# Cross-attention with layer norm: K and V two batches ahead, Q in four groups, the first shift in halves, maxima split behind their transpose

## The chip, the cores and the metric

One core of one Trainium2 chip runs the whole kernel. The metric is the device time in microseconds (us) of one execution. Names: PE is TensorE, DVE is VectorE, ACT is ScalarE, POOL is GpSimd, SP is SyncE, which here only issues transfers.

## The reference

Eight batches, 112 queries, 375 keys, model width 256, 16 heads of 16:

```python
def _attention(query, key_value, W_qkv, b_qkv, W_o, b_o, ln_gamma, ln_beta):
    ...
    Q = (query @ Wq.T + bq).reshape(B, Sq, N_HEADS, D_K).transpose(0, 2, 1, 3)
    K = (key_value @ Wk.T + bk).reshape(B, Skv, N_HEADS, D_K).transpose(0, 2, 1, 3)
    V = (key_value @ Wv.T + bv).reshape(B, Skv, N_HEADS, D_K).transpose(0, 2, 1, 3)
    scores = jnp.einsum('bhqd,bhkd->bhqk', Q.astype(jnp.float32), K.astype(jnp.float32))
    scores = scores / np.sqrt(D_K)
    attn = jax.nn.softmax(scores, axis=-1)
    context = jnp.einsum('bhqk,bhkd->bhqd', attn, V.astype(jnp.float32)).astype(query.dtype)
    context = context.transpose(0, 2, 1, 3).reshape(B, Sq, D_MODEL)
    output = context @ W_o.T + b_o
    x = output + query
    mu = jnp.mean(x, axis=-1, keepdims=True)
    var = jnp.mean(jnp.square(x - mu), axis=-1, keepdims=True)
    return (x - mu) / jnp.sqrt(var + LN_EPS) * ln_gamma + ln_beta
```

## The kernel before, in words

Every engine's program is one list of instructions, written out by the Python code and taken in order; semaphores join the lists. There is no planner: constants say in which unit of a batch a piece of work stands.

**Precision.** Matmul operands for scores and projections are pairs of a rounded high part and a low part (value minus high part), and a product is three matmuls: high by high, high by low, low by high. For the scores the three sit in one contraction: `k_stack` (three buffers, batch b in b % 3) holds high, low, high in every fourth partition, `q_stack` high, high, low. The fourth lane of `k_stack` is filled with ones, and the lanes facing it in `q_stack` take the negated maximum of each query row, the **shift** (its high and its low part). So the softmax's subtraction happens in the matmul.

**Two passes over the scores.** `scores_for_max(n)` (L834; n = 16 b + h is a *head*) computes one head of queries by keys into one of three PSUM banks, and DVE's `head_max(n)` (L656) reduces it to the negated maximum. `negate` (L663, L665) splits the maxima of a batch in high and low part, PE transposes them (`transpose_max`, L841), DVE copies them out of PSUM (`take_shift`, L672) and a transfer issued by ACT puts them in `q_stack` (L520). Then `shifted_scores(i, u)` (L857) computes keys by queries for four heads and a third of the keys: a **unit**, 12 in a batch. ACT takes the exp (L561), and `values` (L873) multiplies with V, which has a column of ones for the denominator; two groups of four heads at a time, in units 1 and 7. The result is copied (`take_o`, L535), transposed (`transpose_o`, job OT, L884), normalised on DVE, transposed back (ONT, L893), copied by ACT (L552), projected (`out_project`, L901) and normalised by row: statistics and rescaling on DVE, the power, gamma and beta on POOL.

**Projections.** `k_project` (two halves of 8 heads a batch), `v_project` (three key chunks) and `q_project` all record line L793. K's half goes through ACT (high part with the bias, L474), DVE (low part, L627) and three transfers of SP into `k_stack` (`stack_k`, L302). Q comes in three groups: batch 0, batches 1 to 4, 5 to 7. The context is split by a cast (L457 on ACT, later L612 on DVE) and a subtraction (L606 on DVE, L359 on POOL).

**Order.** Before batch 0 PE works through 20 heads with Q group 1, V of batch 1, K and V of batch 2 between them (`EARLY_HEADS`, `EARLY_JOBS`). Then `MAX_HEADS` adds 21 heads to the units of batch 0 and 16 to each later batch, and batch i projects K and V of batch i + 3 (`AHEAD`), K in units 0 and 2, V in 3, 5 and 8. Maxima of batch i + 1 are complete by unit 4 or 5 of batch i; the transpose is in unit 7, the shift's transfer behind the exp of unit 9. In batch i stand also OT of batch i - 1 (unit 5), ONT (9) and the output projection (11).

**Banks.** Small results share PSUM banks; `JOBS` lists the order of the jobs of each bank, and `claim` waits until the job before in the same bank has been read (`last_read`).

Of the kernel before, what the change touches and what calls it, by code (L numbers as in the profile page):

```python
# [22 lines left out]
F32 = mybir.dt.float32  # L23
# [9 lines left out]
NC = 3  # L33
# [5 lines left out]
GB = 4  # L39
# [3 lines left out]
Q_STACKS = ((0, 1), (1, 1 + GB), (1 + GB, B))  # L43
# [5 lines left out]
AHEAD = 3  # L49
# [3 lines left out]
Q1_SPLIT = 5  # L53
# [13 lines left out]
EARLY_HEADS = H + 4  # L67
EARLY_JOBS = {1: ("Q", 1, 0), 3: ("Q", 1, 1), 5: ("V", 1, 0), 7: ("V", 1, 1), 9: ("V", 1, 2), 11: ("K", 2, 0),
              13: ("K", 2, 1), 14: ("V", 2, 0), 15: ("V", 2, 1)}


M0_JOBS = [("K", 0, 0), ("V", 0, 0), ("Q", 1, 0), ("K", 2, 0)]
M1_JOBS = [("K", 0, 1), ("V", 0, 1), ("Q", 1, 1), ("K", 2, 1)]
S0_JOBS = [("Q", 0, 0), ("K", 1, 0), ("V", 1, 0), ("MT", 0), ("V", 2, 1)]
S1_JOBS = [("Q", 0, 1), ("K", 1, 1), ("V", 1, 1), ("V", 2, 0)]
for _i in range(B):
    if _i + AHEAD < B:
        M0_JOBS += [("K", _i + AHEAD, 0), ("V", _i + AHEAD, 0), ("V", _i + AHEAD, 1)]
        M1_JOBS.append(("K", _i + AHEAD, 1))
    if _i == 0:  # L80
        M1_JOBS += [("BIAS",), ("Q", 2, 0)]
    if _i >= 1:
        M1_JOBS.append(("OT", _i - 1))
    if _i + 1 < B:
        M1_JOBS.append(("MT", _i + 1))
    if _i == 0:
        M1_JOBS.append(("Q", 2, 1))
    if _i >= 1:
        M1_JOBS += [("ONT", _i - 1), ("OUT", _i - 1)]
M0_JOBS += [("OT_HALF", 0), ("ONT_HALF", 0)]  # L90
M1_JOBS += [("OT_HALF", 1), ("ONT_HALF", 1)]
# [13 lines left out]
def build(nc, x_nat, xT, ctxT, wT, woT, b_cols, bv_cols, b_o, gamma, beta, out):  # L105
    ctx = ExitStack()
    with ctx:
# [63 lines left out]
        shift_in = [sem(f"shift_in{i}") for i in range(2)]  # L171
        stored = [sem(f"stored{i}") for i in range(2)]
# [23 lines left out]
        WIDE = UNITS * (B - 2) + UNITS // 2  # L196
# [15 lines left out]
        def m_job(*job):  # L212
# [35 lines left out]
        def stack_q(queue, k, side):  # L248
# [4 lines left out]
            queue.wait_ge(q_clear[k], 2 if k == 1 else 1)  # L253
# [12 lines left out]
        def _(sp):  # L266
# [76 lines left out]
        def _(pool):  # L343
# [702 lines left out]
```

## Time and profile before

| what | value |
|---|---|
| median of 3 runs | 156.24 us (154.76 to 158.16) |
| profiled execution, time | 157.02 us |
| its span | 155.2 us, granted clock 0.982 on average |
| PE busy | 134.0 us (86%), 1466 matmuls |
| DVE busy | 105.6 us (68%) |
| ACT busy | 80.4 us (52%) |
| POOL busy | 60.7 us (39%) |
| first maximum on DVE starts | 17.1 us |

The span goes from the first to the last instruction; the profiled execution's time is 1.8 us more. Times in rows are us from the span's start. A matmul's busy time overlaps the next one's, so the distance of two starts is the better price. The granted clock is TensorE's, as a share of 2.4 GHz. Batch 3 begins at 82.7 us, batch 5 at 112.6, batch 6 at 123.85 and batch 7 at 135.8.

### The profile page before, as it was taken

Reading aid. Unit: us, or ns where it says so; the run is one execution under the profiler, and the core shown is the slowest. Engines: PE = TensorE matmul, PEld = TensorE weight load, DVE = VectorE, ACT = ScalarE, POOL = GpSimd, SP = SyncE. Lnnn points to the kernel's source line nnn. Section 1 sums busy time; section 2 is a strip of 40 time slices with the busy share of each in tenths; the row PEclk is TensorE's granted clock in tenths of the full one; section 3 lists DMA queues with packets and bytes.
Section 4 is the critical chain, followed back from the end, with each engine's and each line's share of the span. In section 5 each row is a group of like instructions: output and inputs, shape, how many; then the busy total and the mean of one; then the engine's idle time right before and its main releaser. Section 6 shows DMA issues by size and latency. Waiting matters only on the chain.

```text
span 155.2 us, 3853 instructions
## 1 busy us (share of the span) xinstructions
PE 134.0 (86%) x1466; PEld 116.7 (75%) x1466; DVE 105.6 (68%) x247; ACT 80.4 (52%) x163; POOL 60.7 (39%) x83
## 2 busy tenths in 40 slices
PE   5799989679979999889998998999899996779850
PEld 4599779468768899769988987899787875667620
DVE  6745997757937769947896699578779887031252
ACT  3648437214426666526655666465656565566410
POOL 8946997920003998404140504130023023041051
PEclk9999999987999999999999999999999999999997
DMA  4976989698950250697414050405031001001002
GB/s 128 358 259 216 269 296 227 159 270 239 301 204 2 102 156 0 169 267 235 135 52 151 4 178 4 155 2 183 24 128 34 4 4 30 4 4 30 4 0 59
DMA packets 14354, 19.58 MB, mean 126 GB/s; under 512 B 2192, under 2 KB 13520, under 8 KB 14336
## 3 DMA queue, kind: packets, MB, share of 16 engines
q1 hardware_dynamic: 13056, 17.26, 35.6%
q0 software_dynamic: 592, 1.70, 4.5%
q10 hardware_dynamic: 688, 0.38, 0.8%
q8 instruction: 12, 0.20, 0.5%
q14 instruction: 6, 0.05, 0.1%
HBM read 6.30 MB, written 0.92 MB: 47 GB/s over the span
## 4 chain that ended last, share of the span: by engine, by line
PE 65%; DVE 11%; DMA 10%; ACT 6%; issue 5%; SPq 1%; POOLq 0%; ACTq 0%; DVEq 0%
PE m_bank L793 19%; PE pv_bank L873 12%; PE st_bank L857 11%; PE mx_bank L834 10%; DMA q_stack<-shift 6%; DVE mx L656 6%; PE m_bank L901 4%; DMA c_raw<-ctxT 3%; PE m_bank L884 2%; ACT pw L561 2%; PE st_bank L793 2%; DMA q_stack<-q_first 1%; DVE q_hl L618 1%; PE m_bank L841 1%; ACT o_normT L552 1%
## 5 line engine op out<-in xcount | busy, mean ns | idle before, releaser
L656 DVE TENSOR_REDUCE mx<-mx_bank 112x1 f32<-112x375 f32 x128 | 64.6, 541 | 20.4 <-PE mx_bank L834 19.8
L561 ACT ACTIVATE pw<-st_bank 125x448 f32<-125x448 f32 x90 | 48.5, 548 | 48.5 <-PE st_bank L857 47.7
L834 PE MATMUL mx_bank<-k_stack,q_stack 128*112 128x376 f32 x128 | 41.3, 351 | 2.2 <-DVE mx L656 1.2
L857 PE MATMUL st_bank<-q_stack,k_stack 128*125 128x224 f32 x180 | 37.7, 294 | 1.7 <-DMA q_stack<-shift 1.7
L857 PEld LDWEIGHTS st_bank<-q_stack,k_stack 128*125 128x125 f32 x180 | 30.0, 190 | 5.5 <-issue 3.0
L834 PEld LDWEIGHTS mx_bank<-k_stack,q_stack 128*112 128x112 f32 x128 | 22.0, 181 | 4.5 <-DVE mx L656 2.4
L359 POOL TENSOR_TENSOR c_hl<-c_raw,c_hl 128x752 fp32r<-128x752 f32 x6 | 10.9, 1814 | 27.5 <-DVE c_hl L612 27.5
L873 PE MATMUL pv_bank<-pw,v_sb 125*17 125x112 f32 x720 | 20.4, 260 | 1.1 <-ACT o_raw L535 1.1
L405 POOL TENSOR_SCALAR var_eps<-mv 112x1 f32<-112x1 f32 x7 | 1.6, 223 | 49.2 <-DVE mv L692 49.2
L793 PE MATMUL m_bank<-c_hl,w_hl 128*128 128x376 f32 x84 | 18.7, 365 | 0.9 <-ACT w_hl L449 0.9
L873 PEld LDWEIGHTS pv_bank<-pw,v_sb 125*17 125x17 f32 x720 | 16.3, 97 | 3.9 <-issue 2.2
L793 PEld LDWEIGHTS m_bank<-c_hl,w_hl 128*128 128x128 f32 x84 | 16.5, 212 | 1.6 <-ACT c_hl L457 1.6
L793 PE MATMUL m_bank<-w_hl,c_hl 128*125 128x256 f32 x108 | 15.8, 285 | 0.0
L793 PEld LDWEIGHTS m_bank<-w_hl,c_hl 128*125 128x125 f32 x108 | 14.4, 186 | 0.0
L627 DVE SCALAR_TENSOR_TENSOR k_hl<-m_bank,bqk,k_hl 128x376 fp32r<-128x376 f32 x14 | 8.4, 606 | 4.4 <-ACT k_hl L474 4.4
L901 PE MATMUL m_bank<-wo,o_normT 128*112 128x256 f32 x28 | 7.6, 396 | 3.5 <-ACT o_normT L552 3.5
L474 ACT ACTIVATE k_hl<-m_bank,bqk 128x376 fp32r<-128x376 f32 x14 | 8.0, 570 | 2.5 <-PE m_bank L793 2.5
L901 PEld LDWEIGHTS m_bank<-wo,o_normT 128*112 128x112 f32 x28 | 4.4, 176 | 5.5 <-ACT o_normT L552 4.8
L416 POOL TENSOR_TENSOR yo<-z,g_rows 112x256 f32<-112x256 f32 x7 | 5.1, 734 | 7.5 <-DVE z L696 7.5
L688 DVE TENSOR_TENSOR z<-m_bank,x_space 112x256 f32<-112x256 f32 x7 | 2.9, 417 | 6.3 <-PE m_bank L901 6.3
L485 ACT COPY v_sb<-m_bank 125x512 f32<-125x512 f32 (+1 forms) x12 | 5.7, 478 | 1.5 <-issue 1.0
L793 PE MATMUL m_bank<-q_stack,w_hl 128*128 128x448 f32 (+1 forms) x24 | 5.0, 344 | 1.3 <-DVE bo_rows L635 1.3
(102 smaller groups left out, 160.6 us busy)
## 6 DMA issues: line engine op xcount, KB each, us to landing
k_stack<-k_hl SPq DMA_DIRECT2D x48, 188.0 KB, 2.5
c_raw<-ctxT SPq DMA_DIRECT2D x8, 375.0 KB, 4.3
q_stack<-q_hl SPq DMA_DIRECT2D x6, 224.0 KB, 4.5
q_stack<-q_hl SPq DMA_DIRECT2D x6, 168.0 KB, 3.4
x_space<-x_nat POOLq DMA_DIRECT2D x1, 896.0 KB, 10.3
out<-yo SPq DMA_DIRECT2D x8, 112.0 KB, 1.9
pw<-wT SPq DMA_DIRECT2D x2, 256.0 KB, 4.8
x_space<-xT SPq DMA_DIRECT2D x1, 448.0 KB, 6.1
```

What stands on the lines that cost most here:

```text
L359: nc.gpsimd.tensor_tensor(c_hl[b % 2][:, 1, :, :], c_raw[b % 2][:, :, :], c_hl[b % 2][:, 0, :, :].bitcast(F32), op=ALU.subtract).then_inc( ...
L416: nc.gpsimd.tensor_tensor(yo[b % 2][:, :], z[b % 2][:, :], g_rows[:, :], op=ALU.mult).then_inc(y_scaled, 1)
L474: nc.scalar.activation(k_hl[b % 2][:, 0, t, :], src[:, 0:KVP], ACT.Identity, bias=bqk[:, 2 + t:3 + t]).then_inc(k_hi, 1)
L485: nc.scalar.copy(v_sb[b % VR][0:KC, c0:c0 + chunks, :, 0:DK], src[0:KC, 0:chunks * D].rearrange("p (c h d) -> p c h d", c=chunks, h=H)).th ...
L561: nc.scalar.activation(p_tile[0:KC, n % PR, :, :], st_of(n)[0:KC, 0:4 * Q].rearrange("p (j q) -> p j q", j=4), ACT.Exp, scale=float(DK) ** ...
L627: nc.vector.scalar_tensor_tensor(out=k_hl[b % 2][:, 1, t, :], in0=m_bank[m][:, 0:KVP], scalar=bqk[:, 2 + t:3 + t], in1=k_hl[b % 2][:, 0, t ...
L656: nc.vector.tensor_reduce(mx[b % 2][:, h % 2, q_pair(h // 2):q_pair(h // 2) + 1], mx_bank[n % MR][0:Q, 0:KV], axis=AX_X, op=ALU.max, negat ...
L793: last = nc.tensor.matmul(dst, lhs(a, e), rhs(c, e), start=(k + e == 0), stop=(k == len(PRODUCTS) - 1 and e == EC - 1))
L834: nc.tensor.matmul(mx_bank[n % MR][0:Q, 0:KVP], q_stack[k][:, side, q_pair(h // 2), b - Q_STACKS[k][0], :], k_stack[b % 3][:, h // 2, :], ...
L857: last = nc.tensor.matmul(st_of(n)[0:KC, k * 2 * Q:(k + 1) * 2 * Q], k_stack[i % 3][:, 2 * g + k, c * KC:(c + 1) * KC], q_stack[qk][:, :, ...
L873: last = nc.tensor.matmul(pv_of(b, g)[32 * j:32 * j + VW, g * Q:(g + 1) * Q], v_sb[b % VR][0:KC, c, 4 * g + j, :], p_tile[0:KC, (UNITS * b ...
L901: last = nc.tensor.matmul(dst[0:Q, D:2 * D], o_normT[b % 2][:, k, :], wo[:, k, :], start=(k == 0), stop=(k == EC - 1))
```

## The change

- `AHEAD` is 2: batch i projects K and V of batch i + 2, K in units 3 and 5 (4 and 6 in batch 0), V in units 9, 10 and 11. Early heads are 14; K and V of batch 2 are projected in batch 0.
- K's half is read from PSUM once by ACT into `k_full`; ACT copies the high part from there and POOL subtracts the low part. (For the first two batches it is as before.) `stack_k` of a batch waits for all scores of the batch whose buffer it takes.
- The context's high part moves from DVE (unit 7) to ACT (unit 2), and stays one batch ahead of its projection.
- Q has four groups: batch 0, 1 to 2, 3 to 5, 6 to 7.
- Maxima are transposed as they are, and DVE splits them out of PSUM. In later batches their transpose is one job with ONT of batch i - 2. The shift is two transfers issued by SP, one for each part. Batch 0's shift is taken in two halves of 8 heads, the first behind head 9, the second in unit 1 (transfers issued by ACT).
- Output projections and layer norms stand about a batch later: unit 2 of batch i for batch i - 3. The rescaling moves to POOL, the value bias to batch 1.

```diff
-Q_STACKS = ((0, 1), (1, 1 + GB), (1 + GB, B))
+Q_STACKS = ((0, 1), (1, 3), (3, 6), (6, B))
-AHEAD = 3
+AHEAD = 2
-U_K = (0, 2)
-U_V = (3, 5, 8)
-U_OT, U_ONT, U_OUT = 5, 9, 11
-U_BIAS = 4
-U_Q = (5, 10)
-U_NEGATE, U_MT, U_SHIFT = 5, 7, 9
-U_CONTEXT = 7
-HEADS = (1, 1, 2, 1, 2, 1, 1, 1, 2, 1, 2, 1)
+U_OUT, U_OT, U_BIAS, U_Q = 2, 6, 1, 1
+U_K = ((4, 6), (3, 5))
+U_V = ((9, 10, 11), (10, 11, 9))
+NORM_WITH = {3: 0, 4: 1, 5: 2, 6: 3, 7: 5}
+U_MT = (10, 8, 8, 8, 8, 8, 8)
+EARLY_HEADS = 14
+EARLY_JOBS = {1: ("Q", 1, 0), 3: ("Q", 1, 1), 5: ("V", 1, 0), 7: ("V", 1, 1), 9: ("MT", 0, 0), 10: ("V", 1, 2)}
+FIRST_JOBS = {1: (("MT", 0, 1),), 7: (("Q", 2, 0),), 8: (("Q", 2, 1),)}
+HEADS = (2, 2, 2, 1, 2, 1, 2, 1, 1, 1, 1, 0)
+FIRST_HEADS = ((2, 1, 2, 2, 2, 2, 2, 2, 2, 2, 2, 1),)
...
-                    sp.wait_ge(st_full, UNITS * (b - 3) + UNITS // 2 * (t + 1))
+                    sp.wait_ge(st_full, UNITS * (b - 2))
...
+            def stack_shift(b):
+                k = q_stack_of(b)
+                to = q_stack[k][:, :, :, b - Q_STACKS[k][0], :].rearrange("p s a q -> p (s a) q")
+                sp.wait_ge(shift_ready, b + 2)
+                for part in range(2):
+                    row = SPREAD * (part + 1) - 1
+                    sp.dma_start(to[row:row + 1, :, :].bitcast(F32),
+                                 shift[b % 2][:, part, :].bitcast(F32)).then_inc(shift_in[b % 2], 16)
             for i in range(B):
                 if i + AHEAD + 2 < B:
                     load_context(i + AHEAD + 2)
+                if i == 4:
+                    for side in range(2):
+                        stack_q(sp, 3, side)
+                if i + AHEAD < B:
+                    for t in range(2):
+                        stack_k(i + AHEAD, t)
+                if i + 1 < B:
+                    stack_shift(i + 1)
+                if i == 0:
+                    for side in range(2):
+                        stack_q(sp, 2, side)
+                if i >= 3:
+                    store(i - 3)
... (POOL, in its loop)
+            for i in range(B - AHEAD):
+                if i >= 1 and i + AHEAD + 1 < B:
+                    context_lo(i + AHEAD + 1)
+                for t in range(2):
+                    subtract_k(i + AHEAD, t)
+                if i == 0:
+                    context_lo(AHEAD + 1)
... (ACT)
+            def take_k(b, t):
+                src = wait_full(act, "K", b, t)
+                if b > AHEAD:
+                    act.wait_ge(k_lo, 2 * (b - 1) + t + 1)
+                nc.scalar.activation(k_full[:, t, :], src[:, 0:KVP], ACT.Identity,
+                                     bias=bqk[:, 2 + t:3 + t]).then_inc(k_taken, 1)
+                act.wait_ge(k_taken, 2 * (b - AHEAD) + t + 1)
+                act.wait_ge(k_in[(b - 2) % 3][t], 48 * ((b - 2) // 3 + 1))
+                nc.scalar.copy(k_hl[b % 2][:, 0, t, :], k_full[:, t, :]).then_inc(k_hi, 1)
... (DVE)
+            def split_shift(src, to, n):
+                nc.vector.tensor_copy(to[:, 0, :], src).then_inc(shift_hi, 1)
+                dve.wait_ge(shift_hi, n)
+                nc.vector.tensor_tensor(to[:, 1, :], src, to[:, 0, :].bitcast(F32), op=ALU.subtract).then_inc(shift_ready, 1)
... (PE, in shifted_scores)
-                if u == 0:
-                    pe.wait_ge(shift_in[i % 2], 16 * (i // 2 + 1))
+                if i == 0 and u % HALF == 0:
+                    pe.wait_ge(half_in[u // HALF], 32)
+                if i >= 1 and u == 0:
+                    pe.wait_ge(shift_in[i % 2], 32 * ((i + 1) // 2))
```

## Rows read from the trace of the kernel before

**Rows 1.** From the page: the chain that ended last, shares by engine.

```profile
PE 65%; DVE 11%; DMA 10%; ACT 6%; issue 5%; SPq 1%; POOLq 0%; ACTq 0%; DVEq 0%
```

**Rows 2.** Stretches: busy PE, PEld, DVE, ACT, POOL; PEclk, DMA share, GB/s.

```profile
82.70:97.66 14.96, 14.37 (x180) 13.05 (x178) 11.83 (x28) 8.68 (x18) 4.10 (x5) 1.00 0.25 87
112.60:123.85 11.25, 10.90 (x150) 9.01 (x148) 9.90 (x25) 6.67 (x14) 2.24 (x4) 1.00 0.16 55
123.85:135.80 11.95, 9.40 (x141) 7.66 (x139) 6.24 (x18) 6.69 (x14) 2.25 (x4) 1.00 0.04 12
135.80:155.20 19.40, 12.16 (x192) 8.98 (x190) 6.14 (x19) 7.65 (x18) 5.02 (x9) 0.95 0.07 19
28.00:33.00 5.00, 2.39 (x14) 1.53 (x13) 3.66 (x9) 0.96 (x2) 4.00 (x7) 1.00 0.75 193
33.67:37.08 3.41, 3.41 (x15) 3.20 (x14) 1.67 (x4) 1.37 (x3) 0.00 (x0) 0.51 0.92 229
```

**Rows 3.** Timeline of PE in batch 3: start, length, line, idle before it.

```profile
84.74 1.34 PE L873 MATMUL pv_bank<-pw,v_sb 125*17 125x112 f32 x48
86.02 0.48 PE L857 MATMUL st_bank<-q_stack,k_stack 128*125 128x224 f32 x2
...
86.50 1.18 PE L793 MATMUL m_bank<-c_hl,w_hl 128*128 128x376 f32 x6
87.53 0.33 PE L834 MATMUL mx_bank<-k_stack,q_stack 128*112 128x376 f32 x1
87.70 0.37 PE L857 MATMUL st_bank<-q_stack,k_stack 128*125 128x224 f32 x2
87.91 0.34 PE L834 MATMUL mx_bank<-k_stack,q_stack 128*112 128x376 f32 x1
88.08 0.88 PE L793 MATMUL m_bank<-w_hl,c_hl 128*125 128x256 f32 x6
88.80 0.38 PE L857 MATMUL st_bank<-q_stack,k_stack 128*125 128x224 f32 x2
...
96.88 1.09 PE L901 MATMUL m_bank<-wo,o_normT 128*112 128x256 f32 x4 [0.59 <-ACT o_normT L552]
```

**Rows 4.** Groups by line: busy us, mean ns of one, idle before.

```profile
L656 DVE TENSOR_REDUCE mx<-mx_bank 112x1 f32<-112x375 f32 x128 | 64.6, 541 | 20.4 <-PE mx_bank L834 19.8
L359 POOL TENSOR_TENSOR c_hl<-c_raw,c_hl 128x752 fp32r<-128x752 f32 x6 | 10.9, 1814 | 27.5 <-DVE c_hl L612 27.5
L627 DVE SCALAR_TENSOR_TENSOR k_hl<-m_bank,bqk,k_hl 128x376 fp32r<-128x376 f32 x14 | 8.4, 606 | 4.4 <-ACT k_hl L474 4.4
L474 ACT ACTIVATE k_hl<-m_bank,bqk 128x376 fp32r<-128x376 f32 x14 | 8.0, 570 | 2.5 <-PE m_bank L793 2.5
L395 POOL TENSOR_TENSOR x_space<-x_space,bo_rows 112x256 f32<-112x256 f32 x8 | 5.6, 745 | 0.0
L457 ACT CAST c_hl<-c_raw 128x752 fp32r<-128x752 f32 x4 | 3.3, 817 | 1.9 <-DMA c_raw<-ctxT 1.9
L612 DVE CAST c_hl<-c_raw 128x752 fp32r<-128x752 f32 x4 | 2.2, 542 | 0.0
```

**Rows 5.** Tile `k_stack`: its transfers' issues (ns), then all its transfers to landing.

```profile
L302 SPq DMA_DIRECT2D k_stack<-k_hl x48: 529/603/1056, 10.2 to 112.3; - x48
DMA to landing us min/median/max: 2.1/2.5/9.3
```

**Rows 6.** The chain of waits, before batch 0 and before batch 1.

```profile
28.62 0.27 PE st_bank L841
28.91 0.27 DVE shift L672
29.21 3.57 DMA q_stack<-shift
...
49.88 1.99 DMA q_stack<-shift
```

**Rows 7.** From the page: the last constant's transfer, KB and us to landing.

```profile
be_rows<-beta POOLq DMA_DIRECT2D x1, 112.0 KB, 5.6
```

More of the change, by code:

```diff
@@ L38 @@
 UNITS = NG * NC
-GB = 4
+GB = 3
 VW = DK + 1
@@ L74 @@
[L74 to L79, printed above, removed]
+U_OUT, U_OT, U_BIAS, U_Q = 2, 6, 1, 1
+U_K = ((4, 6), (3, 5))
+U_V = ((9, 10, 11), (10, 11, 9))
+HALF = UNITS // 2
+NORM_WITH = {3: 0, 4: 1, 5: 2, 6: 3, 7: 5}
+U_MT = (10, 8, 8, 8, 8, 8, 8)
@@ new lines @@
+EARLY_HEADS = 14
+EARLY_JOBS = {1: ("Q", 1, 0), 3: ("Q", 1, 1), 5: ("V", 1, 0), 7: ("V", 1, 1), 9: ("MT", 0, 0), 10: ("V", 1, 2)}
+FIRST_JOBS = {1: (("MT", 0, 1),), 7: (("Q", 2, 0),), 8: (("Q", 2, 1),)}
+S0_JOBS = [("Q", 0, 0), ("K", 1, 0), ("V", 1, 0), ("MT", 0, 0)]
+S1_JOBS = [("Q", 0, 1), ("K", 1, 1), ("V", 1, 1)]
+M0_JOBS = [("K", 0, 0), ("V", 0, 0), ("Q", 1, 0)]
+M1_JOBS = [("K", 0, 1), ("V", 0, 1), ("Q", 1, 1), ("MT", 0, 1)]
+for _i in range(B - AHEAD):
+    if _i == 1:
+        M1_JOBS.append(("BIAS",))
+    if _i in (2, 3):
+        M0_JOBS.append(("Q", 3, _i - 2))
+    if _i >= 3:
+        M1_JOBS.append(("OUT", _i - 3))
+    M0_JOBS.append(("K", _i + AHEAD, 0))
+    M1_JOBS.append(("K", _i + AHEAD, 1))
@@ L171, in build @@
         shift_in = [sem(f"shift_in{i}") for i in range(2)]
+        half_in = [sem(f"half_in{t}") for t in range(2)]
         stored = [sem(f"stored{i}") for i in range(2)]
@@ L289, in _ @@
             load_x(2)
+            load_x(3)
             load_context(2)
@@ L384, in clear_q, with subtract_k, bias_into_x @@
                 for t in range(2):
-                    wait_full(pool, "Q", 2, t)
+                    wait_full(pool, "Q", 3, t)
                 for side in range(2):
                     for a in range(NP):
-                        last = nc.gpsimd.memset(q_stack[2][:, side, a, :, :].bitcast(F32), 0.0)
-                last.then_inc(q_clear[2], 1)
-            def bias_into_x():
+                        last = nc.gpsimd.memset(q_stack[3][:, side, a, :, :].bitcast(F32), 0.0)
+                last.then_inc(q_clear[3], 1)
+            def subtract_k(b, t):
+                pool.wait_ge(k_hi, 2 * b + t + 1)
+                nc.gpsimd.tensor_tensor(k_hl[b % 2][:, 1, t, :], k_full[:, t, :], k_hl[b % 2][:, 0, t, :].bitcast(F32),
+                                        op=ALU.subtract).then_inc(k_lo, 1)
+            def bias_into_x(half):
                 pool.wait_ge(bias_ready, 1)
                 pool.wait_ge(xb_in, 16)
-                for b in range(B):
+                for b in range(B // 2 * half, B // 2 * (half + 1)):
                     nc.gpsimd.tensor_tensor(xb[:, b, :], xb[:, b, :], bo_rows[:, :], op=ALU.add).then_inc(xb_ready, 1)
@@ L703, in take_bv @@
                 last.then_inc(bv_ready, 1)
-            for n in range(H):
+            for n in range(EARLY_HEADS):
                 head_max(n)
@@ L894, in transpose_o_norm @@
                                                ident[0:Q, 0:Q])
-                last.then_inc(full, 1)
+                return last
+            def transpose_o_norm(b):
+                dst, full = claim("ONT", b)
+                norm_columns(dst, b).then_inc(full, 1)
             def out_project(b):
@@ L997, in _ @@
                         residual()
-                    if u == U_OUT and i >= 1:
-                        out_project(i - 1)
-                    if u in U_V and i + AHEAD < B:
-                        v_project(i + AHEAD, U_V.index(u))
-                    for n in heads[1:]:
-                        scores_for_max(n)
+                    if i + AHEAD < B:
+                        for t in range(2):
+                            if u == U_K[min(i, 1)][t]:
+                                k_project(i + AHEAD, t)
+                        for c in range(NC):
+                            if u == U_V[min(i, 1)][c]:
+                                v_project(i + AHEAD, c)
@@ L1004, in _ @@
+                    for h in heads[1:]:
+                        scores_for_max(h)
             transpose_norm_half(0)
```

341 lines of the change are left out of this document (170 added, 171 removed).

## The prediction

> **What bounds the kernel now.** I read the engine shares first, then the chain of waits, then TensorE's order of work batch by batch. In the table TensorE is busy 86% of the span and no other engine reaches 70%; the chain that ended last is 65% TensorE, 11% VectorE, 10% transfers [rows 1]. So the first question for any reordering is whether TensorE, which takes its instructions in order, meets a new wait. A middle batch shows how little slack there is to win: 14.37 us busy of 14.96 (first of [rows 2]), and the one stall in it is 0.59 us before the output projection (last of [rows 3]). The idle time sits elsewhere: between 28 and 33 us TensorE is busy 2.39 us of 5, then runs 3.41 us at a granted clock of 0.51 (the 1.2 GHz level), and in batches 6 and 7 with the tail it is busy 9.40 of 11.95 and 12.16 of 19.40 us [rows 2]. DVE comes near its limit only in batch 5, 9.90 of 11.25 us.
>
> **Prices on TensorE.** From the starts in [rows 3]: a score unit 0.21 us (87.70 to 87.91), a head for the maxima 0.17 (87.53 to 87.70), half a K projection 1.03, a V chunk 0.72, two groups of values 1.28, an output projection 1.09. A batch is 12 units, 16 heads, 2 K halves, 3 V chunks, 2 pairs of groups and one output projection: 2.5 + 2.7 + 2.1 + 2.2 + 2.6 + 1.1 = 13.2; with the stall of 0.6, 1.2 us are left of the 14.96 for the transposes and the dearer restarts behind values. The same work without the output projection is 13.3 us, and that is my base for a new batch.
>
> **Start, up to batch 1.** Batch 0's first unit now waits at 29.21 for the transfer of the shift, which takes 3.57 us, so batch 0 starts at 32.8; batch 1 starts when the next shift lands, at 51.9 [rows 6]. Moved out of the time before batch 0 are two K halves, three V chunks and 6 heads: 2.1 + 2.2 + 1.0 = 5.3 us. The first half of the shift is taken behind head 9, where the whole was taken behind head 15. Fourteen maxima on DVE from 17.1 (the table), at 0.49 us apart (0.54 each [rows 4], overlapping a little), with the two Q parts (some 0.8) and the split (0.5), end at about 25.3. The half shift leaves near 23.3, in two transfers, one issue (0.6) behind the other, and lands 2 to 3.6 us after the second: 26 to 27.5, and I take 27. So batch 0 starts 6 us earlier with 5.3 us less done: near nothing. The second half is taken in unit 1 and lands about 4.5 us later, in front of unit 6, under the half-clock stretch that I assume to stay.
>
> In batch 0, head 32 (batch 2's first) stands in unit 9 and needs K of batch 2, projected in unit 4. GpSimd must subtract its low part, and GpSimd waits for the constants first. Their last transfer took 5.6 us to land [rows 7] and is now issued behind another memset and a longer row of x parts, so I put the wait's end at 36 to 37 us. Subtraction 1.0, issues 1.2, landing 2.5 to 3.5 us give about 42 us against 40.6 for TensorE's arrival: 1.4 us of stall. Then the transpose of batch 1's maxima stands in unit 10, with some 1.9 us of work behind it, and the shift's way is 0.27 for the transpose, 0.27 for the copy, 0.2 for the new subtraction, 0.62 for the second issue and 1.99 for the landing [rows 6], with gaps 3.6 us: 1.6 us of stall. Batch 1 starts at 46. It is 5.9 us earlier, with 5 heads (0.9), one batch of K and V (4.3), Q's last two parts (1.4) and the value bias (1.1) still to do, 7.7 us. The start loses 1.8 us.
>
> **The K wait, the main term.** The new list of heads has 14 + 22 behind batch 0 and 16 a batch, so in batch i, from 1 to 5, unit 7 holds the first head of batch i + 2. Its K half is projected in unit 3 of the same batch. Before, K came a whole batch earlier. From the start of that projection TensorE has 1.03 for itself, then unit 4 (0.55), unit 5 with the other K half (1.41), unit 6 with the transposes of the outputs (1.0) and unit 7's scores (0.2): 4.2 us. The data need longer:
> - projection 1.03 us;
> - two ACT passes in place of one: 0.57 with bias, then a copy I put at 0.5 (no dearer than the 0.57, and more than half of the 0.82 us that 752 columns take [rows 4]), with the exp of the unit in front and three hand-overs 0.5: 1.6 us;
> - subtraction on GpSimd instead of DVE's 0.61: its passes run 0.75 us for 256 columns and 1.81 for 752 [rows 4], hence 1.0 for 376. Before it in GpSimd's order is the context's low part of 1.81 us, whose high part is now an ACT pass of 0.82 in unit 2; it ends about 0.3 us later than K is ready. 1.3 us;
> - three transfers one behind the other on SP: 2 × 0.60 of issue and 2.1 to 2.5 to land [rows 5]: 3.4 us.
>
> That is 7.3 us against 4.2: 3.1 us, or 2.7 where the output projection in unit 2 lets the context's part finish first. I take 2.7 in all five: **13.5 us**. Nothing covers it: behind the waiting head on TensorE stand its own unit's values and every later unit, so ACT and DVE run dry too. The bounds are 1.5 us a batch (copy and hand-overs at 0.5 together, GpSimd free, landing 2.1) and 3.7 (landing 3.1 while the contexts load). Writing K cannot start earlier: SP waits for all scores of batch i - 1.
>
> **Batches 1 to 5.** The shift's way of 3.6 us has 3.4 us of work behind it (units 8 to 11 with three V chunks): 0.2 a batch. Batch 1 adds the bias (1.1), 2 and 3 half a Q group each (0.7), 3 to 5 an output projection (1.1). Sum: 5 × 13.3 + 13.5 + 1.0 + 1.1 + 1.4 + 3.3 = 86.8; batch 6 starts at 132.8, where it was 123.85.
>
> **Edits that go away.** K's low part (0.61 × 2) and the context's cast (0.54) [rows 4] leave DVE, with the negation and the rescaling, which I put at 0.7 together: 2.5 us a batch, and the 0.59 us stall before the output projection goes, since the transposed outputs now have most of a batch. Only the last is on the path, and it is already out of my base. ACT gains 1.8 us a batch (0.82 and two copies) on 8.68 of 14.96, GpSimd about 2.7 on 4.10 (two subtractions and a rescaling at the 0.75 of 256 columns): both hidden, except in the K chain. The fourth Q group is 12 more matmul pairs, some 0.4 us over all.
>
> **Batch 6 and the end.** Batch 6 has no projection, 12 heads and two output projections: 2.5 + 2.0 + 2.6 + 2.2 + 1.2 = 10.5 us. The last maxima's transpose is in unit 8 with 1.0 us of work behind it, so 2.6 of the shift's 3.6 us are bare, and some of these fall in waits counted already: 12.6 us (11.95 before). From batch 7's start to the end it was 19.40; it now has one more output projection in it: 20.4.
>
> **Sum.** 46.0 + 86.8 + 12.6 + 20.4 = 165.8 us of span. The profiled execution had 155.2 of span and 157.02 of time, so 167.6; that execution is 0.8 above the median of 156.24. I predict **167 us**.
>
> The Trainium skill (DMA: Bandwidth & Descriptors, section Why a DMA increments its semaphore by 16 and not by 1) says that a transfer runs on the largest number of engines, up to 16, that divides the outermost sizes of both its sides. By that the old shift (2 lanes from 32 rows) used 2 engines and the new one 16, so under load it should land nearer 1.99 than 3.57 us; the sum would then be up to 1.6 us lower, all of it at the start.
>
> **Rivals.**
> - *K arrives in time* (0.12). If the way from projection to landing were 4.2 us, not 7.3, the 13.5 us would vanish: 154 us, and 152 with the half shift at its earliest. For it: 2.1 us landings exist [rows 5], and ACT and GpSimd have idle time. Against it: transfer and projection alone make 4.3 us. It decides from a chain under 5 us.
> - *Half the wait* (0.16). Chain near 5.5 us and no stall in batch 0: 167 - 6.5 - 2 = 158 us, no change to be told.
> - *The clock falls too* (0.17). Each K wait is a bare stretch of TensorE. One drop costs half of 3.41 us, 1.7 us [rows 2]; three of five give 172 us, five 176. For it: the drop at 33.67 follows 2.6 us of scattered idle time. Against it: my stalls are that long in the upper half of their range only, and stand between full stretches of work; the 0.59 us stalls [rows 3] bring none.
>
> The Trainium skill (TensorE: Matmul & The Clock Gate, section Part 1: The HAM clock gate) says that the low clock is the default and that only activity lifts it. By that rule the stalls of this change risk the drop in every batch; the trace agrees once, at 33.67.
>
> **Chances and range.** The forecast (a wait of 2 to 3.5 us in each of five batches, clock kept but at the start) has 0.55. A measurement of this kernel tells about 2% from no change, 153.1 to 159.4 us. Faster takes the first rival: 0.12. Within 2% takes the second and loses a little to both sides: 0.15. Slower: 0.73. The range goes from 156, most of the second rival, to 175, the lower bound of the five-drop case.
>
> **What the profile would show.** Right: in batches 1 to 5 an idle time of 2 to 3.5 us before a head matmul in unit 7, released by a transfer into k_stack; batches of 16.8 to 17.8 us; DVE's busy time down by 15 us; no stall before the output projections. Wrong: those matmuls released by nothing, or batches near 14 us. A K wait under 1 us a batch would overturn the forecast; a batch 1 start far from 46 us would shift it by that much.

## The result, and the profile after

The changed kernel takes 180.24 us (median of 4 runs, 178.42 to 180.46) against 156.12 for the kernel before beside it: 1.155 times as long, 95% interval 1.143 to 1.167. Forecast were 167 us and a range from 156 to 175, and the result lies above it. The direction and the main mechanism, the wait for K, are as forecast; 13 us are not. Now and then one execution of the same kernel runs much longer (251.7 us in e7 and 177.8 in p1, where the others took 160 and 163), and the ratios are taken from the fast executions alone.

The page after: busy TensorE, the chain that ended last (the answer to [rows 1]), the granted clock in tenths over 40 slices.

```profile
PE 144.6 (81%) x1479; PEld 124.4 (70%) x1479; DVE 93.0 (52%) x218; ACT 90.7 (51%) x182; POOL 84.0 (47%) x103
...
PEclk9999987999997599969998799999996999558996
...
PE 43%; DMA 18%; POOL 15%; DVE 7%; SPq 6%; ACT 4%; issue 4%; POOLq 0%; ACTq 0%; DVEq 0%
```

TensorE's share of the chain fell from 65% to 43%; transfers, GpSimd and SP's issues have 39% where they had 11%. TensorE's busy time rose by 10.6 us with only 13 more matmuls; in the dips of the clock row each of them takes longer, as the rows of the values below show. By stretches (batches 3, 4, 6, then 7 with the tail; columns as in [rows 2]):

```profile
84.30:104.50 20.20, 17.00 (x184) 14.98 (x184) 10.27 (x24) 10.90 (x23) 10.93 (x24) 0.92 0.25 80
104.50:121.80 17.30, 14.74 (x177) 13.17 (x177) 10.03 (x23) 10.71 (x22) 7.31 (x8) 1.00 0.35 115
...
140.50:156.20 15.70, 12.20 (x152) 10.08 (x150) 9.16 (x23) 7.62 (x17) 6.97 (x10) 0.86 0.02 4
156.20:178.70 22.50, 15.80 (x194) 11.60 (x194) 5.32 (x17) 7.55 (x18) 7.53 (x11) 0.80 0.09 26
```

Batches start at 25.1, 45.2, 65.1, 84.3, 104.5, 121.8, 140.5 and 156.2 us, and the span is 178.7. Batch 3 took 14.96 us before; now 20.2, and batch 4, the one at full clock throughout, 17.3. TensorE's timeline around unit 7 of batches 1, 3 and 4 (start, length, line, idle before it) has the wait:

```profile
57.02 0.65 PE L875 MATMUL mx_bank<-k_stack,q_stack 128*112 128x376 f32 x1 [2.22 <-DMA k_stack<-k_hl]
57.60 2.44 PE L924 MATMUL pv_bank<-pw,v_sb 125*17 125x112 f32 x48
...
93.25 0.65 PE L935 MATMUL m_bank<-ident,o_raw 128*112 128x128 f32 x4 [0.28 <-ACT k_full L512]
...
97.09 0.57 PE L875 MATMUL mx_bank<-k_stack,q_stack 128*112 128x376 f32 x1 [2.81 <-DMA k_stack<-k_hl]
...
116.02 0.42 PE L875 MATMUL mx_bank<-k_stack,q_stack 128*112 128x376 f32 x1 [2.20 <-DMA k_stack<-k_hl]
116.37 1.34 PE L924 MATMUL pv_bank<-pw,v_sb 125*17 125x112 f32 x48
```

The head in front of the values waits for K in each of batches 1 to 5: 2.22, 2.20, 2.81, 2.20, 2.23, in all 11.7 us. Behind it the same 48 matmuls of values take 2.44 us in batch 1 and 1.34 in batch 4 and before (first of [rows 3]): the clock was at its lower level, 1.2 GHz, in one and at 2.4 in the other. The clock falls inside such a wait or within about 1.5 us of its end. The chain that feeds the waiting head, batch 3:

```profile
89.58 1.03 PE m_bank L834 x6
90.62 0.02 issue
90.64 0.58 ACT k_full L512
91.22 0.02 issue
91.25 0.52 ACT k_hl L516
91.76 0.07 issue
91.83 1.01 POOL k_hl L409
...
92.90 0.59 SPq L305
...
93.53 0.60 SPq L305
...
94.17 2.87 DMA k_stack<-k_hl
```

From the projection's start to the landing it is 7.5 us here and 6.9 in the four batches whose last transfer took 2.23 to 2.29 us. And the start, the answer to [rows 6], where batch 1 begins at 45.20:

```profile
30.50 4.28 DMA be_rows<-beta
34.77 0.07 issue
34.85 1.01 POOL k_hl L409
...
37.16 3.56 DMA k_stack<-k_hl
40.72 0.04 issue
40.76 0.44 PE mx_bank L875
...
42.72 0.59 SPq L333
43.31 0.04 issue
43.35 1.80 DMA q_stack<-shift
```

### The profile page after: what moved, and what is told of

The parts are those of the page before. It is cut to its first block, busy times and chain, and to the rows that moved or that the text cites. A ratio compares the mean times of both kernels' runs of the same rounds, so it can differ in the third digit from the quotient of the medians.

```text
span 178.7 us, 3920 instructions
## 1 busy us (share of the span) xinstructions
PE 144.6 (81%) x1479; PEld 124.4 (70%) x1479; DVE 93.0 (52%) x218; ACT 90.7 (51%) x182; POOL 84.0 (47%) x103
## 4 chain that ended last, share of the span: by engine, by line
PE 43%; DMA 18%; POOL 15%; DVE 7%; SPq 6%; ACT 4%; issue 4%; POOLq 0%; ACTq 0%; DVEq 0%
PE pv_bank L924 13%; DMA k_stack<-k_hl 9%; PE m_bank L834 8%; PE st_bank L908 7%; PE mx_bank L875 7%; DMA q_stack<-shift 5%; SPq L305 4%; PE m_bank L955 4%; POOL k_hl L409 3%; DVE mx L700 3%; POOL q_stack L389 3%; DMA be_rows<-beta 2%; DMA c_raw<-ctxT 2%; POOL c_hl L377 2%; SPq L333 2%
## 5 line engine op out<-in xcount | busy, mean ns | idle before, releaser
L875 PE MATMUL mx_bank<-k_stack,q_stack 128*112 128x376 f32 x128 | 44.5, 376 | 14.0 <-DMA k_stack<-k_hl 12.9
L875 PEld LDWEIGHTS mx_bank<-k_stack,q_stack 128*112 128x112 f32 x128 | 22.5, 187 | 17.4 <-DMA k_stack<-k_hl 14.1
L924 PE MATMUL pv_bank<-pw,v_sb 125*17 125x112 f32 x720 | 25.2, 298 | 0.7 <-ACT o_raw L573 0.7
L924 PEld LDWEIGHTS pv_bank<-pw,v_sb 125*17 125x17 f32 x720 | 19.6, 110 | 4.5 <-issue 1.9
L409 POOL TENSOR_TENSOR k_hl<-k_full,k_hl 128x376 fp32r<-128x376 f32 x12 | 12.0, 1002 | 19.5 <-ACT k_hl L516 16.5
L834 PE MATMUL m_bank<-w_hl,c_hl 128*125 128x256 f32 x126 | 19.2, 293 | 0.0
L834 PEld LDWEIGHTS m_bank<-w_hl,c_hl 128*125 128x125 f32 x126 | 17.7, 198 | 0.2
L435 POOL TENSOR_SCALAR yo<-z,mv,rstd 112x256 f32<-112x256 f32 x7 | 8.6, 1234 | 0.8
L512 ACT ACTIVATE k_full<-m_bank,bqk 128x376 f32<-128x376 f32 x12 | 6.9, 576 | 3.3 <-PE m_bank L834 3.3
L487 ACT CAST c_hl<-c_raw 128x752 fp32r<-128x752 f32 x8 | 6.5, 818 | 1.7 <-DMA c_raw<-ctxT 1.7
L516 ACT CAST k_hl<-k_full 128x376 fp32r<-128x376 f32 x12 | 6.1, 506 | 0.4
```

The source lines that it names most:

```text
L409: nc.gpsimd.tensor_tensor(k_hl[b % 2][:, 1, t, :], k_full[:, t, :], k_hl[b % 2][:, 0, t, :].bitcast(F32), op=ALU.subtract).then_inc(k_lo, 1)
L435: nc.gpsimd.tensor_scalar(yo[b % 2][:, :], z[b % 2][:, :], mv[b % 2][:, 0:1], rstd[:, 0:1], op0=ALU.subtract, op1=ALU.mult).then_inc(y_rea ...
L512: nc.scalar.activation(k_full[:, t, :], src[:, 0:KVP], ACT.Identity, bias=bqk[:, 2 + t:3 + t]).then_inc(k_taken, 1)
L834: last = nc.tensor.matmul(dst, lhs(a, e), rhs(c, e), start=(k + e == 0), stop=(k == len(PRODUCTS) - 1 and e == EC - 1))
L875: nc.tensor.matmul(mx_bank[n % MR][0:Q, 0:KVP], q_stack[k][:, side, q_pair(h // 2), b - Q_STACKS[k][0], :], k_stack[b % 3][:, h // 2, :], ...
L924: last = nc.tensor.matmul(pv_of(b, g)[32 * j:32 * j + VW, g * Q:(g + 1) * Q], v_sb[b % VR][0:KC, c, 4 * g + j, :], p_tile[0:KC, (UNITS * b ...
```

## Experiments

Times are medians; ratios are to the kernel before, measured beside each. A ratio is mostly known to 1 or 1.5%, so a step of 1 or 2 us between two versions is within the noise. Batch lengths and waits come from the one profiled execution of each.

**e1: the first head that needs the new K, two units later** (unit 9 in place of 7).

```diff
-HEADS = (2, 2, 2, 1, 2, 1, 2, 1, 1, 1, 1, 0)
+HEADS = (2, 2, 2, 1, 2, 1, 2, 0, 0, 1, 1, 2)
```

> One constant of the changed kernel: the heads of units 7 and 8 move to unit 11 (2,2,2,1,2,1,2,0,0,1,1,2), so batch i + 2's first head stands in unit 9 and K has 2.9 us more. Theory A (the K wait, and the low clock that follows it, are the loss): no wait for k_stack in batches 1 to 5 (11.7 us less), full clock there (the stretches at half clock in these batches are 17 us long and cost about 8), so about 160 us. Theory B (the work moved to ACT and GpSimd has become a bound of its own, the K wait only shows it first): the wait returns elsewhere, about 172 us or more.

168.5 us, 1.078 (1.066 to 1.090). Half of the excess is gone, so the wait is real and costs; but the expected 160 us are not reached, as it went in batches 2 and 4 only. The chain of waits has the last K transfer of batches 1, 3 and 5 at:

```profile
53.91 4.07 DMA k_stack<-k_hl
88.94 4.00 DMA k_stack<-k_hl
122.49 3.66 DMA k_stack<-k_hl
```

where it lands 1.4 to 1.8 us later than the 2.3 of the changed kernel, and the wait is back at 2.00, 1.77 and 1.44 us. Behind the first two the clock fell once more, and not behind the third: the second wait, and the clock row of the page (4.2 us a digit; the dips at the 15th, 23rd and 24th stand for 58 to 62 and 91 to 100 us).

```profile
92.99 0.43 PE L875 MATMUL mx_bank<-k_stack,q_stack 128*112 128x376 f32 x1 [1.77 <-DMA k_stack<-k_hl]
...
PEclk9999995999999969999999789999999999969995
```

Queues' packets while batch 1's transfer is under way (packets, MB, share of 16 engines' time), first e1, 53.9 to 58.0 us:

```profile
q1 hardware_dynamic: 621, 0.84, 57.4%
q8 instruction: 1, 0.02, 2.3%
```

and the changed kernel, 54.7 to 57.0 us:

```profile
q1 hardware_dynamic: 512, 0.70, 84.3%
```

In e1 the data queue is nearly empty from 55.0 to 56.5 us, behind one packet of 16 KB on an instruction queue that took 1.5 us. In e1, e2 and the changed kernel, a packet of that queue starts within each K transfer in this chain that took 3.6 us or more in batches 1 to 5 (six of them) and within none of those that took 2.2 to 2.9 (seven). e8 and e9, further down, add six late ones (3.56 to 4.15 us), each with such a packet. That is a coincidence without exception, not an experiment on it.

**e2: one unit later** (unit 8).

```diff
+HEADS = (2, 2, 2, 1, 2, 1, 2, 0, 1, 1, 1, 1)
```

> The same list with the first head of batch i + 2 in unit 8 (2,2,2,1,2,1,2,0,1,1,1,1), 1.6 us later than in the changed kernel. Theory A: waits of 0.6 to 1.2 us in batches 1 to 5, too short to bring the clock down: 4 to 5 us over the version with unit 9, about 164 us. If any stall brings the clock down, whatever its length, it stays above 170 us.

172.2 us, with runs from 168.3 to 175.5, too wide for a ratio, and above the expected 164. The waits are 2.30, 0.52, 2.24, 0.53 and 2.33 us, with landings of 4.04, 2.23, 3.95, 2.29 and 4.03. One unit hides the wait to 0.5 us, as the sum has it, where no instruction packet falls into the transfer. The clock fell behind each of the three long waits and behind neither of the short ones.

**e3: thirteen filler matmuls in front of the wait** into the bank of the waiting head, which overwrites them.

```diff
+                if h == 0 and b >= 3:
+                    pe.wait_ge(max_read, n - MR + 1)
+                    kb = q_stack_of(b - 2)
+                    for f in range(FILL):
+                        nc.tensor.matmul(mx_bank[n % MR][0:Q, 0:KVP], ...)
                 if h % (H // 2) == 0:
                     pe.wait_ge(k_in[b % 3][h // (H // 2)], 48 * (b // 3 + 1))
```

> The changed kernel, with 13 matmuls of an earlier batch's head (0.17 us each, 2.2 us) before the wait for K in batches 1 to 5, into the bank that the real head then overwrites: TensorE works through the wait, which stays as long. It prices the clock alone. Theory A with the clock as its second half: full clock in batches 1 to 5, 8 us less, about 171 us. If the low clock costs nothing (the work after the wait has slack): 179 us.

175.2 us, 1.111 (1.097 to 1.125). The filler does no useful work and the kernel is 5 us faster than the changed one. The stretches from the end of the K wait to the next batch (batches 1 and 4, and the sum over 1 to 5), first the changed kernel:

```profile
57.02:65.10 8.08, 8.08 (x80) 7.11 (x81) 2.53 (x6) 2.43 (x5) 1.03 (x2) 0.63 0.22 65
...
116.02:121.79 5.77, 5.71 (x81) 5.10 (x81) 2.53 (x6) 2.77 (x7) 1.98 (x3) 1.00 0.25 84
...
sum 35.55, PE 35.28 PEld 30.93 DVE 12.84 ACT 13.53 POOL 10.84; mean PE 7.06 PEld 6.19 DVE 2.57 ACT 2.71 POOL 2.17
```

and e3:

```profile
57.83:63.66 5.83, 5.50 (x80) 4.87 (x80) 2.53 (x6) 2.70 (x6) 0.33 (x1) 1.00 0.16 56
...
111.77:117.60 5.83, 5.72 (x82) 5.12 (x81) 2.53 (x6) 2.83 (x7) 2.02 (x3) 1.00 0.25 84
...
sum 29.10, PE 28.37 PEld 25.30 DVE 12.64 ACT 13.96 POOL 9.42; mean PE 5.67 PEld 5.06 DVE 2.53 ACT 2.79 POOL 1.88
```

The same 81 matmuls take 5.8 us at full clock, in all five batches of e3 and in the one of the changed kernel that kept it, and 7.1 to 8.1 in the other four. The difference of the sums, 6.5 us, is the price of the clock in batches 1 to 5: 2.25 us for the stretch of 6.8 us at the lower level in batch 1, and 1.3 to 1.6 us for each of the three others, of about 3.4 us.

**After again**, the changed kernel unedited.

> The changed kernel once more, beside the versions made from it, so that their differences are taken on one chip: 180 us, with K waits of 2.2 to 2.9 us in batches 1 to 5, as in its profile. If the clock's part is left to chance by run, its profile shows another set of half-clock stretches and the same waits.

179.8 us. The K waits repeat to a hundredth or two (2.24, 2.21, 2.81, 2.22, 2.21), the low clock does not: it comes behind the waits of batches 2 and 5 alone, and twice about the change to batch 7.

```profile
PEclk9999995799999999987999999999996999678996
```

A wait of 2.2 us sometimes brings it down and sometimes not. In the four executions with such waits (the two of this kernel, e2 and t2 below) the clock fell behind 13 of the 18 K waits of 2.2 to 2.8 us. The start does not repeat either: the low stretch there lasts 7 us in place of 3.4, K of batch 2 takes 4.77 us to land in place of 3.56, and batch 1 starts at 46.84.

**e4: K's low part on DVE as before,** without the second ACT pass and the subtraction on GpSimd.

```diff
-                        take_k(i + AHEAD, U_K[min(i, 1)].index(u))
+                        k_hi_part(i + AHEAD, U_K[min(i, 1)].index(u))
-                    subtract_k(i + AHEAD, t)
+                        k_lo_part(i + AHEAD, U_K[min(i, 1)].index(u - 1))
```

> Undoes one part of the change: K's half is read from PSUM by ACT and DVE as before (one ACT pass of 0.57, one DVE pass of 0.61), without the copy on ACT and the subtraction on GpSimd. The chain loses the copy 0.5, GpSimd's 1.0 and its wait, and gains 0.61: K waits near 1.1 us instead of 2.2 to 2.8. Theory A: 6 us less by the waits, and the clock, if it then holds, 8 us more: 165 us, 172 if it falls all the same. Theory B: GpSimd and ACT relieved, so at least as low as the version with unit 9.

170.0 us, 1.076 (1.059 to 1.093). TensorE's waits, in total, times, longest:

```profile
PE m_bank L935 <- DVE k_hl L669: 5.8, 5, 1.2
...
PE mx_bank L875 <- DMA k_stack<-k_hl: 3.0, 5, 0.6
```

The K wait falls from 11.7 to 3.0 us, and a new one of 5.8 stands beside it: OT shares a bank with K's second half and now has to wait for DVE to read it. Once in the five batches, in batch 1, the clock fell all the same, behind waits of 1.16 and 0.61 us that stand within 2.8 us.

**e5: e4 and e1 together.**

> Both edits that shorten the K wait together: K's low part on DVE as before, and the first head of batch i + 2 in unit 9. The chain is about 1.2 us shorter and the head 2.9 us later, so no wait even where a K transfer lands in 4 us in place of 2.3, as it did in batches 1, 3 and 5 with the heads in unit 9 alone. Theory A: batches 1 to 5 at 15.5 to 16.5 us, the whole at 161 us; what is then left over the kernel before (5 us) stands at the start and in batch 6. Theory B: 168 us, as either edit alone.

164.3 us, 1.060 (1.051 to 1.069). No wait for K is left in batches 1 to 5, which last 15.6, 16.1, 16.2, 16.3 and 15.5 us, OT's 1.16 each included. The 3 us over the expected 161 stand outside them: a wait of 2.38 us for K in batch 0, where its last transfer took 7.25 us, one of 2.37 for the shift of batch 7, and low clock behind both.

**e6: the last maxima earlier.** The twelve last heads in units 0 to 5 of batch 6, their transpose in unit 7.

```diff
+    _l = ... HEADS if _i < 6 else (2,) * 6 + (0,) * 6
-U_MT = (10, 8, 8, 8, 8, 8, 8)
+U_MT = (10, 8, 8, 8, 8, 8, 7)
```

> The version before, and in batch 6 the last 12 heads two by two in units 0 to 5 and the transpose of the last maxima in unit 7 in place of 8. The waits there (1.7 us for the last maximum, 2.4 for the last shift) should fall to 0.5 and 1.0: 2.5 us less, 158.5 us. If DVE bounds batch 6 in any order of its heads, no change.

161.0 us, 1.032 (1.021 to 1.044). Batch 6 takes 13.0 us where it took 15.3. The reason is in the changed kernel's timeline, batch 6 and the start of batch 7:

```profile
150.42 0.47 PE L908 MATMUL mx_bank<-q_stack,k_stack 128*125 128x224 f32 x2 [1.72 <-DVE mx L700]
...
156.17 1.18 PE L908 MATMUL st_bank<-q_stack,k_stack 128*125 128x224 f32 x4 [1.78 <-DMA q_stack<-shift]
```

From unit 8 of batch 6 the shifted scores use a bank of the maxima as a third one, and so wait for DVE's last heads; then the shift is late too.

**t2 and t1: the same edit alone, without and with e3's filler.**

> The changed kernel with the twelve last heads in the first six units of batch 6 and their transpose in unit 7 instead of 8; nothing else. It was worth 2.3 us of batch 6 where the clock stood (15.3 to 13.0). Here, by the sum, 180.2 - 2.3 = 177.9 us. If the late maximum and shift of batch 6 also bring the clock down, as in the changed kernel's profile from 151.5 us on, batch 7 gains another 2.7 us (22.4 to 19.7): 175 us.

> The same with the thirteen filler matmuls in front of each wait for K. With filler alone the time was 175.2 us and the clock full from batch 1 on, so only batch 6's own 2.3 us are left to gain: 172.9 us. If it is 170 or less, batch 6's wait had cost a clock drop in most runs of the filler kernel too.

176.0 us, 1.127 (1.115 to 1.140), and 172.6 us, 1.112 (1.102 to 1.122). The tail edit is worth 4.2 us without filler and 2.6 with it: batch 6 falls to 12.9 and 13.7 us, and batch 7 is at 19.7 in both. Without filler the edit should also give back the clock of the tail (22.5 to 19.7 us in the profiles), but the 1.6 us between the two are no more than the noise. In t2 the K waits are those of the changed kernel, and the clock fell behind four of the five, the first four. The filler is worth 3.4 us here, less than the 6.5 read above; part of the rest is its own doing, as in e3 and t1 TensorE still waits 0.7 to 0.9 us for K behind the filler in batch 1, and e3 0.9 in batch 5.

**e7, e8, e9: the rest of the way back.** e7 puts OT in the other bank, e8 takes batch 2's first head to unit 11 of batch 0, e9 takes the first head of batch i + 2 to unit 10.

```diff
-        M1_JOBS.append(("OT", _i - 1))
+        M0_JOBS.append(("OT", _i - 1))
...
-FIRST_HEADS = ((2, 1, 2, 2, 2, 2, 2, 2, 2, 2, 2, 1),)
+FIRST_HEADS = ((2, 1, 2, 2, 2, 2, 2, 2, 2, 1, 0, 4),)
...
-HEADS = (2, 2, 2, 1, 2, 1, 2, 0, 0, 1, 1, 2)
+HEADS = (2, 2, 2, 1, 2, 1, 2, 0, 0, 0, 2, 2)
```

> The last kernel with the outputs' transposes (job OT) in the other PSUM bank, where the job in front is K's half 0 of unit 3 and not half 1 of unit 5. If the 1.16 us before these transposes is only the wait for DVE to read K's half 1 out of that bank, it goes in all five batches: batches 1 to 5 at 15.0 instead of 16.2 us, no wait over 0.3 us before OT, and 161.0 - 5.8 = 155.2 us. If the data of the transposes, or DVE's order, are late as well, part of the wait comes back at the transposes or at the next maxima: 158 us or more.

> The same with the first head of batch 2 moved from unit 9 to unit 11 of batch 0. If the stall of 2.4 us at 41.8 us is bare time of its own, the transpose of batch 1's maxima comes 2 us earlier and batch 1 starts 2 us earlier, at 44.5 to 45: 153.2 us. If K of batch 2 lands just as late for unit 11 (about 44 us), or the shift's transfer is late for another reason, it moves 1 us at most: 154.5 us.

> The mended kernel with the first head of batch i + 2 in unit 10 instead of 9. The profile before it had waits for K of 1.3, 1.6 and 1.1 us in batches 1, 3 and 5, where the third transfer landed in 3.6 to 4.1 us. If they are bare time, they go: 158.9 - 4.0 = 155 us, a shade under the kernel before. If two heads each in units 10 and 11 crowd DVE in front of the next batch, or the shift becomes the late one (3.0 us to land in batches 2 and 4), half comes back: 157 us.

159.8 us, 1.025 (1.012 to 1.038); 158.9, 1.018 (1.004 to 1.032); 155.5, **0.994 (0.988 to 0.999)**. e7 gained 1.3 us, not 5.8, and the waits of e8, which has the same bank, say why:

```profile
PE mx_bank L876 <- DMA k_stack<-k_hl: 3.9, 3, 1.6
```

OT's wait is gone, but TensorE comes to the head that much sooner, and K, with an instruction packet in each of the three transfers again, is late: 4 us came back. e8 moved batch 1's start from 46.85 (e6) to 44.96 and gained 0.9, not clear of the noise. e9's waits in batches 1 to 5, and its batches 4 and 6:

```profile
PE mx_bank L876 <- DMA k_stack<-k_hl: 2.0, 3, 0.9
PE st_bank L909 <- DMA q_stack<-shift: 1.5, 2, 0.8
```

```profile
93.20:107.40 14.20, 14.20 (x178) 13.27 (x178) 10.97 (x25) 9.43 (x19) 5.31 (x6) 1.00 0.45 147
...
122.20:135.10 12.90, 11.32 (x150) 9.35 (x149) 9.54 (x24) 7.79 (x16) 5.98 (x9) 1.00 0.03 9
```

Batches 1 to 5 are 15.3, 15.7, 15.8, 14.2 and 14.8 us. So with the order mended the kernel is level with the one before: 0.6% less, between 0.1 and 1.2. It is no longer the whole change, as K's low part is back on DVE.

**p1 and p2: the split of the maxima alone, in the kernel before.** p1 transposes the maxima as they are, lets DVE split them out of PSUM, and sends the shift in two transfers from ACT; p2 has only the two transfers.

```diff
-                act.dma_start(q_stack[k][SPREAD - 1:2 * SPREAD:SPREAD, :, :, b - Q_STACKS[k][0], :] ...
+                for part in range(2):
+                    row = SPREAD * (part + 1) - 1
+                    act.dma_start(to[row:row + 1, :, :].bitcast(F32), ...
```

> One part of the change alone, put into the kernel before: the maxima are transposed as they are and DVE splits them out of PSUM, and the shift goes in two transfers (of ACT) in place of one. My prediction put this at nothing. The negation leaves DVE before the transpose (0.35 us) and one subtraction (0.26) comes behind it, with 0.6 for the second issue: the shift lands 0.9 us later in quiet stretches, hidden by the 1.5 to 3 us that TensorE has in hand there, and earlier under load if the single transfer was slow for its shape. Expected 156.5 us; 159 if the later landing is exposed in every batch.

> The kernel before with nothing changed but the shift's transfer in two, one for each part, both issued by ACT. If the 4% that the split behind the transpose cost with such transfers are the second issue on ACT (0.6 us in front of ACT's copies, once a batch) and a later landing, this kernel shows most of it: 160 to 162 us. If they come from where DVE splits, this one stays at 156.5 us or below, since the skewed first landing of 3.57 us falls to about 2 us by the number of engines.

> The kernel before with the maxima transposed unsplit, split by DVE out of PSUM, and two transfers on ACT, once more for a profile. Time 163 us as before. If the two issues on ACT carry it, the profile shows 0.9 us before each output projection in place of 0.59 and batches 0.5 to 1 us longer in batches 1 to 6; if the first shift carries it, only the start of batch 0 moves, by 1 to 2 us.

p1 163.2 and 162.9 us, 1.041 (1.027 to 1.055) and 1.038 (1.013 to 1.063); p2 163.5, 1.052 (1.040 to 1.063). The expected 156.5 us are missed by 7. The two transfers alone carry all of it; where DVE splits costs nothing that shows. In p2's chain of waits the first shift, and in its timeline one of the output projections (the answers to [rows 6] and the last of [rows 3]):

```profile
30.14 5.40 DMA q_stack<-shift
```

```profile
102.46 1.09 PE L903 MATMUL m_bank<-wo,o_normT 128*112 128x256 f32 x4 [1.12 <-ACT o_normT L554]
```

Batch 0 starts at 35.7 in place of 32.9, and the stall before the output projection is 1.1 us in place of 0.59: ACT issues a second transfer (0.6 us) in front of its copy. A third part is the clock: in p2 it stood at the lower level from 34.5 to 41.3 us, in the kernel before from 33.7 to 37.1, and batch 0 took 20.3 us in place of 19.0. In the changed kernel SP issues them, and nothing waits behind.

## Why the prediction was right, and where it was wrong

**The start was right.** Forecast were a half shift landing at 27, a stall of 1.4 us for K behind the constants, one of 1.6 for the shift, and batch 1 at 46. Measured: 25.1, 1.27, 1.49 and 45.2. GpSimd's wait for the constants ended at 34.85, not 36 to 37, but K's landing took 3.56 us. Batch 0 started 1.9 us early and was 1.1 longer. The 0.8 us between forecast and profile mean little: the changed kernel once more started batch 1 at 46.84, and the other versions with this start at 44.4 to 47.5.

**The main term was right in place and cause,** and e1, e2 and e4 shorten it by three different edits, and e5 removes it. It was 11.7 us for 13.5. The chain was 6.9 us (7.5 in batch 3) for 7.3: two ACT passes 1.2 for 1.6, GpSimd 1.0 for 1.3 as K did not wait for the context's part (in batch 1 the two were ready within 0.03 us of each other), issue and landing 3.6 (4.2 in batch 3) for 3.4. The cover was 4.7 for 4.2, so 2.2 a batch and 2.8 in batch 3.

**The step that failed is "clock kept but at the start".** I had the mechanism as a rival (the clock falls too, 0.17), priced at 1.7 us a drop, and spoke against it because only the upper half of my stalls reached the 2.6 us of idle time before the drop at 33.67, because they stood between full stretches of work, and because those of 0.59 brought none. The first reason did not even fit my own figure of 2.7 us a batch. The granted clock fell behind four of the five waits in one profile and two of five in the other, once for 6.8 us. In batches 1 to 5 it cost 6.5 us (e3's stretches), and with batch 7's 2.8 us (22.5 against e3's 19.7) 9 of the missing 13. The argument against it compared with 0.59 us and had nothing between 0.59 and 2.6; e1 has two waits in between, 2.00 and 1.77 us, and the clock fell behind both. The rule of the Trainium skill that I had quoted (TensorE: Matmul & The Clock Gate, section Part 1: The HAM clock gate: the low clock is the default, activity lifts it) was the better guide; the trace now agrees, for K waits of 2.2 to 2.8 us 13 times in 18, and for e1's of 2.00 and 1.77 us.

**The second is "batch 6, 12.6 us":** 15.7, and 15.3 at full clock. I put 2.1 us of bare shift and missed that unit 8's scores go into a bank of the maxima and wait 1.72 us for DVE's last heads, before the shift is late by 1.78. e6 and t2 bring it to 13.0 and 12.9.

**The third is small, "batches 1 to 5, 13.3 a batch":** 3.8 us over my sum without clock and K waits (95.3 measured, less 86.8, plus 1.8, less 6.5). The stall of 0.28 before OT, for the bank that ACT still reads, costs 0.44 a batch between starts (0.61 from the head before to OT, 0.17 in e9), 2.2 in all; the head behind a wait takes 0.35 and not 0.17, 0.9 in all; 0.7 stays open.

| span, us | forecast | measured | difference |
|---|---|---|---|
| start of batch 1 | 46.0 | 45.2 | -0.8 |
| K waits, 1 to 5 | 13.5 | 11.7 | -1.8 |
| clock, 1 to 5 | 0 | 6.5 | +6.5 |
| rest of 1 to 5 | 73.3 | 77.1 | +3.8 |
| batch 6 | 12.6 | 15.7 | +3.1 |
| batch 7 and tail | 20.4 | 22.5 | +2.1 |
| sum | 165.8 | 178.7 | +12.9 |

Batch 7's 20.4 was right but for the clock: 19.7 wherever the clock stays full. The row of batch 6 holds 0.4 us of the clock too (15.7 against 15.3).

**The rule of the Trainium skill that I weighed for the two shift transfers** (DMA: Bandwidth & Descriptors, section Why a DMA increments its semaphore by 16 and not by 1) counts engines, and from 2 engines against 16 I took "nearer 1.99 than 3.57" us. No view here shows how many engines a transfer used. The times fit without load (1.80 to 1.83 us for the last landing, against 1.99) and not under it: 5.40 and 4.49 us in p2 and p1 against 3.57. But the second transfer also leaves 0.9 us later, into a stretch where the DMA engines were busier (a share of 0.90 and 0.81, against 0.65), so the number of transfers and the load are not told apart. The measurement decides against the rule as I used it.

**Signatures.** K waits of 2.2 to 2.8 us in unit 7: as forecast. No stall before the output projections: right. DVE down by 15: 12.6. Batches of 16.8 to 17.8 us: in this profile only batch 4, where the clock stayed. The prices that GpSimd had: 1.0 us a subtraction (1.0 taken), but 1.23 for a rescaling, for which I had taken 0.75; it lay under other work.

The two groups:

```profile
L409 POOL TENSOR_TENSOR k_hl<-k_full,k_hl 128x376 fp32r<-128x376 f32 x12 | 12.0, 1002 | 19.5 <-ACT k_hl L516 16.5
...
L435 POOL TENSOR_SCALAR yo<-z,mv,rstd 112x256 f32<-112x256 f32 x7 | 8.6, 1234 | 0.8
```

## What to carry to other kernels

When a reordering shortens the lead of a producer, price the wait as the chain from producer to landing less the consumer's work in between. Then price what the wait does to TensorE's clock: here 1.3 to 1.6 us for each stretch of about 3.4 us at the lower level, behind 13 of the 18 K waits of 2.2 to 2.8 us. One wait of the same length behind which the clock stood is no proof that it will stand. A wait that goes shows the next one: here K, then the bank of OT, then K again, so add up the slack of all consumers behind it before counting the gain. Look at who owns the bank that a unit writes, not only at who owns its inputs.

## What the runs showed of the hardware

- In batches 1 to 5 of the changed kernel, e1, e2, e8 and e9, an instruction packet of 16 KB, taking about 0.8 to 1.5 us, coincides with each K transfer in the chain of waits that lands in 3.6 to 4.2 us, and with none of those that land in 2.2 to 2.9.
- K waits of 2.2 to 2.8 us brought the granted clock down after two of five in one execution and four of five in another of the same kernel, and 13 times in 18 over four executions; waits of 2.00 and 1.77 us did so too in e1. Matmuls of no use in the gap kept it at full and made the kernel 5 us faster.
- Two small transfers in place of one took 0.9 to 1.8 us longer to land in a busy stretch (not measured at the same load), and the kernel before took 5% longer with them (1.040 to 1.063), with their second issue and a longer stretch of low clock in that.
- What remains open: 0.7 us of batches 1 to 5, why the same 2.2 us wait lowers the clock only at times, whether the instruction packets cause the late landings, and whether two transfers would land later at the same load.
